# Two weight splits of the second routed expert moved ahead of the slot scatters on GpSimd

## The chip, the cores and the metric

One core of one Trainium2 chip. The metric is device time in microseconds, median of three runs. A profiled execution of the same kernel gives the trace.

## What is computed

Patch embedding, one attention layer and one mixture-of-experts layer over 16 images of 69 tokens (1 class token, 36 patches, 32 text tokens), so T = 1104 tokens of width 256:

```python
h = tok(x)                                   # layernorm, 768 -> 256, layernorm, position table
h = concatenate([h, txt], axis=1)
h = h + attn(layernorm(h))                   # one head, rotary, width 256
n = layernorm(h)
shared = gelu(n @ shared_up) @ shared_down   # 256 -> 1024 -> 256
probs = softmax(n @ router_w)                # 8 experts, top 2
routed = sum over the top 2 of prob * (gelu(n @ up[e]) @ down[e])
out = h + shared + routed + n
```

## The kernel before

The engines run programs of their own and meet at semaphores. Each matrix product in the expert part is done as three products of a high and a low part (split_product, lines 791 to 797), so each weight half of 128x2048 numbers (`w_up` or `w_dn` of one expert) is split on GpSimd once it has landed in `stage`: `hi` is a rounded copy (line 346, tensor_scalar), `lo` the rest (line 347, tensor_tensor). The results go into `ring`, which has RING = 3 places of two halves each. Expert 0 is the shared one, 1 to 8 are routed.

`prepare_half(x, part)` (line 354) splits one half, tells `w_free`, and issues by `load_weights` (line 331) the load of the half that is two further on in the list. At part 1 it also tells `w_ready`, on which TensorE waits before the expert's first product. From x = 3 on it waits first until the place in the ring is free: for x = 3 until the shared expert is done (`ffn_done` of 1), for later ones until the expert three before has had its last tile.

The shared expert is done in 3 groups of 384 tokens by 8 pieces of 128 hidden columns, n = 0 to 23: TensorE makes the up product (shared_up), ScalarE the gelu into `gact` (line 593), VectorE splits it into `hid` (lines 1142 and 1143), TensorE adds the down product (line 844) of three pieces earlier. At the end of each group VectorE adds the result to `base` (line 1151).

Routing is woven into it. VectorE takes the softmax and the two best experts of each token (lines 1210 to 1236; ScalarE does the exp of line 611 in between), TensorE counts tokens before each by 18 small products (line 892), and VectorE makes of them the slot of each token at its expert (lines 1245 to 1260). On its semaphore `r_slots` (line 1260) GpSimd starts 18 scatters (line 477), each of up to 128 token rows from `hx` to `slots` in HBM. SP waits for all of them (line 304) and reads the slots back in tiles of 128 into `xg`.

Then come TILES = 25 routed tiles: TensorE transposes xg and does up, transposes of the hidden tile, and down; ScalarE and VectorE empty PSUM in between (lines 619, 642, 650, 1288, 1311), VectorE scales by the gate into `y_all` (line 1318). GpSimd adds each tile to the output by an accumulating indirect DMA (line 493), in a loop that stands behind all prepare_half calls, and waits between some of them for the earlier ones to have landed.

The order on GpSimd's own queue around the change is written out by hand: split(1, 0), prepare_half(1, 1), the waits for `slots_init` and `r_slots`, the 18 scatters, prepare_half of x = 2 to 8, the additions.

Of the kernel before, what the change touches and what calls it, by code (L numbers as in the profile page):

```python
# [50 lines left out]
NX = NE + 1  # L51
# [8 lines left out]
def fusion_layer(nc, patches, txt, cls_token, cls_pos, ln1_gb, tok_w, tok_bias, ln2_g, ln2_b,  # L60
# [16 lines left out]
    with ctx:  # L77
# [245 lines left out]
        def _(pool):  # L323
# [7 lines left out]
            def load_weights(n):  # L331

                if n < 2 * NX:
                    if n >= 2:
                        pool.wait_ge(w_free, n - 1)
                    pool.dma_start(stage[:, n % 2, :], (w_up, w_dn)[n % 2][n // 2, :, :]).then_inc(w_in[n % 2], 16)

            def tiles_before(x):

                return pool.value_load(tend_int[0:1, x - 1:x], min_val=0, max_val=TILES)  # L340

            def split(x, part, c0, c1):

                pool.wait_ge(w_in[part], 16 * (x + 1))
                hi, lo = (ring[:, x % RING, v, UPW * part + c0:UPW * part + c1] for v in range(2))
                link(nc.gpsimd.tensor_scalar(hi, stage[:, part, c0:c1], 1.0, 0.0, ALU.mult, ALU.add))  # L346
                return nc.gpsimd.tensor_tensor(lo, stage[:, part, c0:c1], hi.bitcast(F32), ALU.subtract)  # L347

            def turn_done(x):

                pool.wait_ge(w_free, 2 * x + 2)
                pool.sem_inc(w_ready, 4)  # L352

            def prepare_half(x, part):

                if x > RING and part == 0:

                    pool.wait_ge(ffn_done, tiles_before(x - RING) + 1)
                    pool.sem_inc(slot_free, 1)
                elif x == RING and part == 0:  # L360

                    pool.wait_ge(ffn_done, 1)
                split(x, part, 0, UPW).then_inc(w_free, 1)
                if part == 1:
                    turn_done(x)
                load_weights(2 * x + part + 2)
# [61 lines left out]
            def flat_bases(g):  # L428
                for i in flat_tiles_after(g):
                    pool.wait_ge(f_normed, i + 1)  # L430
                    r = ROWS[i]
                    nc.gpsimd.tensor_tensor(base[0:r, i, :], h2f[0:r, i % NBUF_FLAT, :], hx[0:r, i, 0:D],
                                            ALU.add).then_inc(f_base, 1)
# [35 lines left out]
            load_weights(4)  # L469
            flat_bases(NG)  # L470
            prepare_half(1, 1)

            pool.wait_ge(slots_init, 32)
            pool.wait_ge(r_slots, 1)
            for i in range(NT):
                for k in range(2):
                    pool.indirect_dma_start(  # L477
                        slots_d, bass.IndirectOffsetOnAxis(ap=slot_i[0:ROWS[i], k, i:i + 1].bitcast(U32), axis=0),
                        hx[0:ROWS[i], i, :], None).then_inc(slots_out, 16)
            for x in range(2, NX):  # L480
                for part in range(2):
                    prepare_half(x, part)

# [892 lines left out]
```

## Time and profile before

| | us |
|---|---|
| median of 3 runs | 402.31 |
| lowest, highest | 398.47, 403.0 |
| profiled execution | 403.5 |
| its span, first to last instruction | 401.5 |

The profiled execution had a mean granted TensorE clock of 0.902 of full speed. In the rows below a line of a timeline has the start in us, the duration in us, engine, line of the program, operation, what is written and read, the count, and in brackets the idle time before it with what ended it.

### The profile page before, as it was taken

Reading aid. Unit: us, or ns where it says so; the run is one execution under the profiler, and the core shown is the slowest. Engines: PE = TensorE matmul, PEld = TensorE weight load, DVE = VectorE, ACT = ScalarE, POOL = GpSimd, SP = SyncE. Lnnn points to the kernel's source line nnn. Section 1 sums busy time; section 2 is a strip of 40 time slices with the busy share of each in tenths; the row PEclk is TensorE's granted clock in tenths of the full one; section 3 lists DMA queues with packets and bytes.
Section 4 is the critical chain, followed back from the end, with each engine's and each line's share of the span. In section 5 each row is a group of like instructions: output and inputs, shape, how many; then the busy total and the mean of one; then the engine's idle time right before and its main releaser. Section 6 shows DMA issues by size and latency. Waiting matters only on the chain.

```text
span 401.5 us, 6810 instructions
## 1 busy us (share of the span) xinstructions
PE 312.3 (78%) x2019; PEld 278.8 (69%) x2020; DVE 229.4 (57%) x494; ACT 118.1 (29%) x239; POOL 239.0 (60%) x164
## 2 busy tenths in 40 slices
PE   0895939865895699808778999989999999999600
PEld 0673837764783499807767898979999999998500
DVE  2588889996779968309696345452475342423200
ACT  1464422511322231100132343424242434343000
POOL 1587548756258804789285058589987755466341
PEclk9999769998697679957898999999999999999965
DMA  8926390411320322225325103335434235344322
GB/s 232 242 54 215 130 288 23 132 49 36 134 89 7 110 93 81 107 84 170 109 73 210 40 15 128 121 120 194 157 118 131 41 43 78 50 52 52 42 26 26
DMA packets 22995, 41.17 MB, mean 103 GB/s; under 512 B 2622, under 2 KB 19456, under 8 KB 20672
## 3 DMA queue, kind: packets, MB, share of 16 engines
q0 software_dynamic: 7056, 24.46, 22.5%
q1 hardware_dynamic: 15264, 15.93, 14.7%
q10 hardware_dynamic: 656, 0.55, 0.4%
q8 instruction: 10, 0.16, 0.2%
q14 instruction: 9, 0.07, 0.1%
HBM read 29.01 MB, written 11.90 MB: 102 GB/s over the span
## 4 chain that ended last, share of the span: by engine, by line
PE 36%; DVE 22%; DMA 20%; issue 8%; POOL 6%; another core or an unknown queue 3%; POOLq 2%; ACT 1%; SPq 0%; DVEq 0%; ACTq 0%
DMA out_tokens<-y_all,dest 10%; PE ps L794 8%; PE ps L795 8%; PE ps L796 8%; DMA h_after_attention<-h 5%; PE ps L660 5%; PE ps L844 5%; DVE hid L1143 4%; DVE hid L1142 2%; POOL ring L347 2%; DMA xp<-in_patches 2%; POOLq L490 2%; DMA h2f<-h_after_attention 2%; DVE qk L1040 1%
## 5 line engine op out<-in xcount | busy, mean ns | idle before, releaser
L347 POOL TENSOR_TENSOR ring<-stage,ring 128x2048 fp32r<-128x2048 f32 (+1 forms) x21 | 84.7, 4032 | 1.8
L493 POOL DMA_INDIRECT out_tokens<-y_all,dest x25 | 39.1, 1565 | 40.5 <-DMA out_tokens<-y_all,dest 33.2
L1311 DVE TENSOR_TENSOR hgT<-ps,hgT 128x512 fp32r<-128x512 f32 x50 | 32.2, 686 | 53.3 <-ACT hgT L650 53.3
L794 PE MATMUL ps<-ring,hgT 128*128 x200 | 58.0, 290 | 2.1 <-DVE y_all L1318 1.5
L346 POOL TENSOR_SCALAR ring<-stage 128x2048 fp32r<-128x2048 f32 (+1 forms) x21 | 36.6, 1742 | 34.5 <-PE ps L796 24.7
L795 PE MATMUL ps<-ring,hgT 128*128 x200 | 56.0, 280 | 0.0
L796 PE MATMUL ps<-ring,hgT 128*128 x200 | 55.9, 280 | 0.0
L844 PE MATMUL ps<-ring,hid 128*128 128x256 f32 x216 | 33.2, 304 | 15.5 <-DVE base L1151 12.1
L642 ACT ACTIVATE hg<-ps 128x512 f32<-128x512 f32 x50 | 29.9, 598 | 51.3 <-PE ps L796 51.3
L794 PE MATMUL ps<-ring,xgT 128*128 x100 | 42.2, 422 | 2.1 <-POOLq L352 1.0
L844 PEld LDWEIGHTS ps<-ring,hid 128*128 128x128 f32 x216 | 31.6, 211 | 16.5 <-issue 12.3
L796 PE MATMUL ps<-ring,xgT 128*128 x100 | 40.2, 402 | 0.0
L795 PE MATMUL ps<-ring,xgT 128*128 x100 | 40.1, 401 | 0.0
L794 PEld LDWEIGHTS ps<-ring,hgT 128*128 128x128 f32 x200 | 37.6, 188 | 2.6 <-issue 2.6
L795 PEld LDWEIGHTS ps<-ring,hgT 128*128 128x128 f32 x200 | 37.6, 188 | 0.0
L796 PEld LDWEIGHTS ps<-ring,hgT 128*128 128x128 f32 x200 | 37.5, 187 | 0.0
L1318 DVE TENSOR_SCALAR y_all<-ps,gate 128x256 f32 (+1 forms) x25 | 12.1, 484 | 39.0 <-PE ps L796 39.0
L593 ACT ACTIVATE gact<-ps 128x384 f32<-128x384 f32 x24 | 11.8, 492 | 65.8 <-DVE hid L1143 25.7
L477 POOL DMA_INDIRECT slots<-hx,slot_i x18 | 17.8, 990 | 21.5 <-DVE tend_int L1260 16.3
L650 ACT ACTIVATE hgT<-ps 128x512 fp32r<-128x512 f32 x50 | 27.1, 598 | 2.6 <-PE ps L660 2.6
L1143 DVE TENSOR_TENSOR hid<-gact,hid 128x384 fp32r<-128x384 f32 x24 | 26.3, 1095 | 0.8
L619 ACT ACTIVATE xgT<-ps 128x256 fp32r<-128x256 f32 x25 | 9.6, 385 | 56.4 <-PE ps L660 56.4
(167 smaller groups left out, 681.0 us busy)
## 6 DMA issues: line engine op xcount, KB each, us to landing
stage<-in_w_up POOLq DMA_DIRECT2D x9, 1024.0 KB, 5.2
stage<-in_w_dn POOLq DMA_DIRECT2D x9, 1024.0 KB, 5.2
slots<-gact SPq DMA_DIRECT2D x1, 3262.5 KB, 14.5
xg<-slots SPq DMA_DIRECT2D x25, 130.5 KB, 2.1
xp<-in_patches SPq DMA_DIRECT2D x6, 288.0 KB, 7.9
h_after_attention<-h SPq DMA_DIRECT2D x4, 276.0 KB
h2f<-h_after_attention SPq DMA_DIRECT2D x8, 128.0 KB, 2.1
ring<-in_tok_w SPq DMA_DIRECT2D x1, 768.0 KB, 6.4
```

The lines of the kernel that those rows point to most:

```text
L346: link(nc.gpsimd.tensor_scalar(hi, stage[:, part, c0:c1], 1.0, 0.0, ALU.mult, ALU.add))
L347: return nc.gpsimd.tensor_tensor(lo, stage[:, part, c0:c1], hi.bitcast(F32), ALU.subtract)
L493: pool.indirect_dma_start(out, bass.IndirectOffsetOnAxis(ap=dest[:, t:t + 1].bitcast(U32), axis=0), y_all[:, t, :], None, compute_op=ALU.a ...
L642: nc.scalar.activation(hg[:, 1 - c, 512 * half:512 * (half + 1)], ps[:, hidden_bank + half, :], ACT.Gelu).then_inc(e_act, 1)
L650: nc.scalar.activation(hgT[:, c, 0, 4 * half:4 * half + 4, :], ps[:, turned_bank + half, :].rearrange("p (k t) -> p k t", k=4), ACT.Copy). ...
L660: return nc.tensor.transpose(o, i, ident[0:n, 0:n])
L794: nc.tensor.matmul(o, a[0], b[0], start=n == 0, stop=False)
L795: nc.tensor.matmul(o, a[0], b[1], start=False, stop=False)
L796: last = nc.tensor.matmul(o, a[1], b[0], start=False, stop=n == len(pairs) - 1)
L844: last = nc.tensor.matmul(ps[:, down_bank[j], 0:D], a[x], b[y], start=f == 0 and m == 0, stop=f == KF - 1 and m == 2)
L1143: v.tensor_tensor(hid[:, 1, f, :], gact[:, n % 2, :], hid[:, 0, f, :].bitcast(F32), ALU.subtract).then_inc(s_lo, 1)
L1311: v.tensor_tensor(hgT[:, c, 1, 4 * half:4 * half + 4, :], ps[:, turned_bank + half, :].rearrange("p (k t) -> p k t", k=4), hgT[:, c, 0, 4 ...
```

## The change

Both halves of expert 2 are split directly behind those of expert 1, ahead of the waits for `slots_init` and `r_slots` and ahead of the scatters. The loop behind the scatters begins at expert 3. With each half the issue of a load moves too: that of `w_up[3]` and of `w_dn[3]`. No wait and no operation is added or dropped.

```diff
             flat_bases(NG)
             prepare_half(1, 1)
+            prepare_half(2, 0)
+            prepare_half(2, 1)
 
             pool.wait_ge(slots_init, 32)
             pool.wait_ge(r_slots, 1)
@@
-            for x in range(2, NX):
+            for x in range(3, NX):
                 for part in range(2):
                     prepare_half(x, part)
```

## Rows read from the trace of the kernel before

**Rows 1.** Timeline of GpSimd, the last expert's splits, the first and last addition
```profile
303.43 1.90 POOL L346 TENSOR_SCALAR ring<-stage 128x2048 fp32r<-128x2048 f32 x1 [2.05 <-PE ps L796]
...
311.99 4.61 POOL L347 TENSOR_TENSOR ring<-stage,ring 128x2048 fp32r<-128x2048 f32 x1
317.56 1.68 POOL L493 DMA_INDIRECT out_tokens<-y_all,dest  x1 [0.96 <-DVE y_all L1318]
...
394.64 1.56 POOL L493 DMA_INDIRECT out_tokens<-y_all,dest  x1 [2.86 <-DMA out_tokens<-y_all,dest]
```

**Rows 2.** Timeline of VectorE, the last tile of y
```profile
379.46 0.48 DVE L1318 TENSOR_SCALAR y_all<-ps,gate 128x256 f32<-128x256 f32 x1 [4.15 <-PE ps L796]
```

**Rows 3.** Timeline of TensorE, its one wait for weights in the routed tiles
```profile
269.58 0.49 PE L794 MATMUL ps<-ring,xgT 128*128 x1 [1.02 <-POOLq L352]
```

**Rows 4.** Timeline of GpSimd, 133 to 209 us: splits, load, scatters
```profile
133.50 4.53 POOL L347 TENSOR_TENSOR ring<-stage,ring 128x2048 fp32r<-128x2048 f32 x1
138.62 0.60 POOL L336 DMA_DIRECT2D stage<-in_w_dn  x1 [0.59 <-POOL ring L347]
155.53 1.17 POOL L477 DMA_INDIRECT slots<-hx,slot_i  x1 [16.31 <-DVE tend_int L1260]
...
177.62 0.90 POOL L477 DMA_INDIRECT slots<-hx,slot_i  x1 [0.30 <-issue]
...
188.06 4.56 POOL L347 TENSOR_TENSOR ring<-stage,ring 128x2048 fp32r<-128x2048 f32 x1
...
203.92 4.63 POOL L347 TENSOR_TENSOR ring<-stage,ring 128x2048 fp32r<-128x2048 f32 x1
```

**Rows 5.** The page, DMA issues: count, size, median from issue to landing
```profile
stage<-in_w_dn POOLq DMA_DIRECT2D x9, 1024.0 KB, 5.2
```

**Rows 6.** Timeline of VectorE beside GpSimd's splits, and once without
```profile
133.66 4.78 DVE L1143 TENSOR_TENSOR hid<-gact,hid 128x384 fp32r<-128x384 f32 x1
...
139.61 0.56 DVE L1143 TENSOR_TENSOR hid<-gact,hid 128x384 fp32r<-128x384 f32 x1
...
188.23 4.80 DVE L1143 TENSOR_TENSOR hid<-gact,hid 128x384 fp32r<-128x384 f32 x1
...
204.08 0.35 DVE L1299 TENSOR_REDUCE ytab<-ecmp 1x25 f32<-1x200 f32 x1
204.47 4.13 DVE L1300 SCALAR_TENSOR_TENSOR ytab<-small,rtab 1x25 f32<-1x25 f32 x1
```

**Rows 7.** Timeline of VectorE, the routing chain up to the slot numbers
```profile
142.48 0.23 DVE L1220 TENSOR_TENSOR rout<-rout,rsm 128x72 f32<-128x72 f32 x1
...
145.90 0.17 DVE L1236 TENSOR_SCALAR hx<-rsm 128x9 f32<-128x9 f32 x1
...
151.35 0.17 DVE L1245 COPY rtab<-ps 128x8 f32<-128x8 f32 x1 [0.18 <-PE ps L892]
...
154.45 0.16 DVE L1260 CAST tend_int<-rtab 1x8 int32<-1x8 f32 x1
```

**Rows 8.** Timeline of TensorE: the counting products, two restarts after idle time, the last shared products
```profile
149.20 2.11 PE L892 MATMUL ps<-rsel,mats 128*128 128x72 f32 x18
...
182.44 2.26 PE L844 MATMUL ps<-ring,hid 128*128 128x256 f32 x9 [12.05 <-DVE base L1151]
...
193.08 2.29 PE L844 MATMUL ps<-ring,hid 128*128 128x256 f32 x9 [2.40 <-DVE hid L1143]
...
200.45 1.30 PE L844 MATMUL ps<-ring,hid 128*128 128x256 f32 x9
```

**Rows 9.** Windows of TensorE: length, busy (instructions), granted clock, DMA share, GB/s
```profile
182.40:186.00 3.60, 3.56 (x14) 0.50 0.59 184
...
193.00:196.50 3.50, 3.42 (x14) 0.52 0.54 169
```

**Rows 10.** Timelines of ScalarE and of VectorE, the stall inside the scatters
```profile
179.74 0.49 ACT L593 ACTIVATE gact<-ps 128x384 f32<-128x384 f32 x1 [10.77 <-remote]
...
181.21 1.08 DVE L1151 TENSOR_TENSOR base<-base,ps 128x256 f32<-128x256 f32 x3 [11.26 <-remote]
```

## The prediction

> **What bounds the kernel now.** I read the page first, then the timelines of GpSimd, VectorE, TensorE and ScalarE between 120 and 215 us, then the tail, because the page shows no engine full over the whole span and the reader has to find, stretch by stretch, which one the others wait for.
>
> The tail belongs to GpSimd. It issues the 25 accumulating DMAs of line 493 only when all weight splits are done: the last split starts at 311.99 us and takes 4.61, the first addition starts at 317.56 and the last at 394.64 [rows 1]. VectorE had the last tile of y ready at 379.46 + 0.48 us [rows 2], 15 us before its addition, and the same holds for every addition before it, so the additions are a fixed string of 77 us hung on the end of the splits. The splits of the eighth routed expert start at 303.43 us, after 2.05 us of idling for TensorE [rows 1]: they wait for the last tile of the fifth. TensorE runs tile behind tile up to there, with one wait worth a name, 1.02 us at 269.58 [rows 3]. So what moves the start of the routed phase moves the end one to one. That start is the end of the shared expert (201.75 us: 200.45 + 1.30, the last products of line 844 [rows 8]), followed by a stretch in which VectorE is held up behind the split of expert 3, which is itself released by the end of the shared expert. Everything hangs on when TensorE finishes the shared expert.
>
> Before that lies the routing: VectorE's chain of small operations to the slot numbers (line 1260 at 154.45), 18 scatters on GpSimd from 155.53 to 178.52, one each 1.27 us [rows 4], and then x = 2's two splits, which this change moves.
>
> **What is removed, added, moved.** Nothing is removed. Two halves of work move to the front of the wait for the slot numbers. Each is a tensor_scalar of 1.90 us [rows 1] and a tensor_tensor of 4.5 us [rows 4], with the load of the half after the next (0.60 us of issue [rows 4]). Their data are there: the first half was requested before the splits of expert 1 ended, the second at 138.62 [rows 4], and such a load lands 5.2 us after its issue [rows 5]. From 139.26 I get: first tensor_scalar to 141.2, tensor_tensor 141.25 to 145.8, 0.3 gap, issue to 146.7, second pair 146.75 to 148.66 and 148.75 to 153.3, wait and issue to 154.5. That is 15.2 us in an idle gap of 16.31 us [rows 4]. On GpSimd alone the edit costs nothing, since the slot numbers come 154.6 us; with that cover gone it would cost up to 15.2 us. The two extra loads (7 and 6 of the list) move ahead of the scatters with it; they use the queue while nothing else does, and their 5.2 us are over before the first scatter. SP's queue is passed by nothing; what waits on it for the scatters are the reads of xg.
>
> **The cost: VectorE while GpSimd splits.** Three operations show it. VectorE's line 1143 (two inputs from SBUF) takes 0.56 us alone, 4.78 us at 133.66 beside GpSimd's tensor_tensor of 133.50, and 4.80 at 188.23 beside that of 188.06; it ends 0.4 us after GpSimd's [rows 4, 6]. Small size does not save it: the 1x25 operation of line 1300 takes 4.13 us at 204.47 and ends with the split of 203.92 (4.63 us). The tensor_reduce of line 1299 at 204.08, inside that same split, takes 0.35 and is not held [rows 4, 6]. The Trainium skill (SBUF — State Buffer, Who interferes with whom) says the same of two-input operations and of reduces; it adds that who issues first keeps the port and the other waits, which is a rival below.
>
> So I walk VectorE's chain through the four new GpSimd operations, letting one held operation in at each boundary. Line 1142 of n = 7 (139.22 before) ends at 141.4. Its line 1143 waits for 145.8 and ends at 146.2. The maximum and the subtraction (lines 1210, 1211; input from PSUM) run, ScalarE's exp answers, lines 1213 and 1214 run; line 1215 has two SBUF inputs and waits for 148.66; line 1219 is a reduce; line 1220 waits for the last split and ends at 153.5. Before, it ended at 142.71 [rows 7]. From there nothing holds the chain: +10.8 us. The mask (end of line 1236, 146.07 before [rows 7]) is at 156.9.
>
> TensorE's 18 small products of line 892 took 2.11 us at full clock from 149.20 [rows 8]. They now start at 157.0, after TensorE has idled some 5 us: its shared steps run out of finished pieces at about 151.4, as n = 8 of ScalarE also waits behind the late exp. After idle times of 12 and 2.4 us the granted clock was 0.50 and 0.52 (1.2 GHz) for the next 3.5 us [rows 8, 9]; at that clock the products take 4.4 us and end at 161.4. The other end, full clock, gives 159.3. I take the slow one. VectorE's line 1245 moves from 151.35 to 161.6: **+10.2 us** (other end 8.3), and so do the slot numbers (154.61 to 164.8) and the scatters: 165.7 to 188.7.
>
> **The stall inside the scatters.** Between about 170 and 180 us ScalarE, VectorE and TensorE all stand still. ScalarE idles 10.77 us until 179.74, VectorE 11.26 us until 181.21, both on an unnamed releaser, though the products they need ended at 167.2 and 168.3 by the trace [rows 10]; TensorE waits 12.05 us for VectorE [rows 8]. It ends about 1.2 us after GpSimd's last scatter (177.62 + 0.90). No row names the cause. I take it to belong to the scatters, since it begins well inside them and ends with them: the change then shifts it whole, to 190-191. TensorE's distance from its line 892 to the first scatter stays 4.3 us, so it gets as far before the stall as now.
>
> **The gain.** After the stall TensorE needs 182.44 to 201.75 = 19.3 us. In it lie 2.40 us of waiting for line 1143, held by the second half's split, and then 3.5 us at clock 0.52 [rows 8, 9], which loses half of them, 1.7. With the splits gone from there both vanish: **-4.1 us**, leaving 15.2. The other holds of VectorE in this stretch lie under TensorE's slow-clock work and pay nothing. TensorE ends the shared expert at 192.6 + 15.2 = 207.8 instead of 201.75. Tiles 0 and 1 of xg are there by then: read from about 191.4 on, and even at the 5.2 us of the larger weight load [rows 5] landed by 197. Expert 2's weights are ready at 154 instead of 194, but TensorE asks for them only after the tiles of expert 1, and it has no wait there now: no gain. GpSimd waits for TensorE at the split of expert 3 before and after, so the earlier end of the splits is idle time there.
>
> **Sum:** +10.2 - 4.1 = +6.1 us on the span of 401.5, so 407.6; the profiled execution was 403.5 and the median of three is 402.31, which makes 408.4 by the latter. About 1% (4 us) is what a measurement of this kernel can tell.
>
> **Rivals.**
> A, the forecast, 0.56: 408.4. With full clock at line 892: +8.3 - 4.1 = +4.2, 406.5. If TensorE is one shared step (2.1 us) less far when the stall begins: 410.5. Own range 405.5 to 411.
> B, the stall does not come back, 0.13: TensorE goes on from 161.4 with 13 steps of 2.1 us (line 844's nine products take 2.26 at half clock [rows 8], so 1.1 at full, the up products as long) and three lone down products, 3.4 us: 192.4. It must also have xg: scatters end 188.7, and a larger load lands in 5.2 [rows 5], so at most 193.9, then two down products, 196. I take 194.5, between these, against 201.75. -7.2 us, 395.1. For it: the stall has no named releaser; against it: the same scatters run beside the same work. It decides the sign as soon as more than 6 of the 12 us are gone.
> C, VectorE is first at the port and keeps the chain moving, 0.12: the chain's operations take 0.23 us, and if each is let in ahead of GpSimd, the slot numbers come as now, and only the -4.1 remains: 398.2. For it: VectorE's operations are many and short; against it: in every case in rows 4 and 6 the VectorE operation waited for the whole of GpSimd's. The page of the skill named above supports either, by order of issue, and gives no price here.
> D, between, 0.19: the holds cost half (some small operations slip in, or line 1220 falls into the gap of 0.9 us between the halves), or part of the stall is absorbed: +5 - 4.1 or +10.2 - 10: about 0 to +3.5, 402 to 406.
>
> **Numbers.** The likeliest is 408.4. Above 411.5 I leave 0.07, below 397.5 0.10 (most of B): range 397.5 to 411.5. Slower by over 1%: nearly all of A and some of D, 0.55. Within 1%: most of D, the mild edge of A and of C, 0.22. Faster: B, most of C, 0.23.
>
> **What would show it.** In the changed profile: four GpSimd splits between 139 and 154; line 1143 of n = 7 near 4.9 us and line 1220 near 4.7; line 1245 near 161.6; TensorE's line 892 at about twice 2.1 us; first scatter near 165.7; a stall of about 10 us on ScalarE ending near 190; no wait of TensorE for line 1143 after it; first split of expert 3 near 208; first addition near 323.6. Wrong if line 1260 stays under 158 (C), or if ScalarE has no unnamed wait over 5 us (B).

## The result

The changed kernel takes 407.36 us (median of 4, 405.68 to 409.7), the kernel before 401.34 (median of 4, 398.47 to 403.0): ratio 1.0138, 95% interval 1.0084 to 1.0192, so about 6 us slower. In a later pair of the same two programs it was 405.2 against 400.31, ratio 1.0145 (1.0063 to 1.0227). All medians here take every execution, while the ratios leave out those over 1.5% above the fastest of their kernel, so a ratio can differ a little from the quotient of the medians beside it.

The profiled execution of the changed kernel is its fastest one, 405.68, with a span of 403.7 us, against 401.5 before: 2.2 us in the two traces for 6 us in the medians. That gap needs an explanation of its own, below.

The lines that were added move the ones below: what was line 1142 is 1144 here, 1143 is 1145, 1220 is 1222, 844 is 846, 890 is 892, 892 is 894, 1283 is 1285. First GpSimd's timeline, to be read beside [rows 4]: start, duration, operation, and idle time before it.

```profile
139.25 1.91 POOL L346 TENSOR_SCALAR ring<-stage 128x2048 fp32r<-128x2048 f32 x1
141.25 4.76 POOL L347 TENSOR_TENSOR ring<-stage,ring 128x2048 fp32r<-128x2048 f32 x1
146.31 0.58 POOL L336 DMA_DIRECT2D stage<-in_w_up  x1 [0.30 <-POOL ring L347]
146.92 1.91 POOL L346 TENSOR_SCALAR ring<-stage 128x2048 fp32r<-128x2048 f32 x1
148.92 4.55 POOL L347 TENSOR_TENSOR ring<-stage,ring 128x2048 fp32r<-128x2048 f32 x1
...
165.61 1.17 POOL L479 DMA_INDIRECT slots<-hx,slot_i  x1 [10.97 <-DVE tend_int L1262]
...
187.44 0.90 POOL L479 DMA_INDIRECT slots<-hx,slot_i  x1 [0.30 <-issue]
207.72 1.90 POOL L346 TENSOR_SCALAR ring<-stage 128x2048 fp32r<-128x2048 f32 x1 [19.38 <-PEq L908]
```

The splits fit into the former gap, but GpSimd still idles 10.97 us for the slot numbers, and the first scatter is 10.1 us later. The time saved on GpSimd behind the scatters appears as 19.38 us of waiting for the shared expert. VectorE's timeline shows what made the slot numbers late (beside [rows 6, 7]):

```profile
138.77 2.81 DVE L1145 TENSOR_TENSOR hid<-gact,hid 128x384 fp32r<-128x384 f32 x1
141.50 4.73 DVE L1144 CAST hid<-gact 128x384 fp32r<-128x384 f32 x1
...
148.08 0.84 DVE L1217 TENSOR_TENSOR rout<-rout,rsm 128x72 f32<-128x72 f32 x1
148.96 0.23 DVE L1221 TENSOR_REDUCE rsm<-rout 128x9 f32<-128x72 f32 x1
149.22 4.33 DVE L1222 TENSOR_TENSOR rout<-rout,rsm 128x72 f32<-128x72 f32 x1
...
161.44 0.17 DVE L1247 COPY rtab<-ps 128x8 f32<-128x8 f32 x1 [1.82 <-PE ps L894]
```

Each held operation ends 0.1 to 0.4 us after the GpSimd operation beside it (141.58, 146.23, 148.92 and 153.55 against 141.16, 146.01, 148.83 and 153.47); a product of 72 numbers per partition takes 4.33 us instead of 0.23, and the reduce between two held ones takes its 0.23. The longest hold, 4.73 us, is of a cast, which has only one SBUF input. TensorE, beside [rows 8]; the line ACT is ScalarE's gelu of n = 16, with the stall in front of it:

```profile
156.97 0.71 PE L892 MATMUL ps<-rsel,mats 128*128 128x80 f32 x2 [5.13 <-DVE hx L1238]
157.47 3.93 PE L894 MATMUL ps<-rsel,mats 128*128 128x72 f32 x18
...
185.69 0.49 ACT L595 ACTIVATE gact<-ps 128x384 f32<-128x384 f32 x1 [9.46 <-remote]
186.33 0.66 PE L796 MATMUL ps<-hT_n,ring 128*128 128x384 f32 x1 [6.66 <-issue]
...
194.06 1.26 PE L846 MATMUL ps<-ring,hid 128*128 128x256 f32 x9 [0.70 <-DVE base L1153]
...
206.23 1.30 PE L846 MATMUL ps<-ring,hid 128*128 128x256 f32 x9
```

The counting products take 3.93 us, not 2.11, at a granted clock of 0.50 (157 to 161.5 us) behind an idle time of 5.13. The shared expert is done at 207.53, 5.8 us later than before (201.75). From 194.06 on no wait for line 1145 is left.

### The profile page after: what moved, and what is told of

It reads as the page before. It is cut to its first block, busy times and chain, and to the rows that moved or that the text cites. A ratio compares the mean times of both kernels' runs of the same rounds, so it can differ in the third digit from the quotient of the medians.

```text
span 403.7 us, 6810 instructions
## 1 busy us (share of the span) xinstructions
PE 314.8 (78%) x2019; PEld 280.5 (69%) x2020; DVE 227.2 (56%) x494; ACT 117.9 (29%) x239; POOL 238.9 (59%) x164
## 4 chain that ended last, share of the span: by engine, by line
PE 35%; DVE 24%; DMA 19%; issue 7%; POOL 6%; another core or an unknown queue 4%; POOLq 2%; ACT 1%; SPq 0%; DVEq 0%; ACTq 0%
DMA out_tokens<-y_all,dest 10%; PE ps L796 8%; PE ps L798 8%; PE ps L797 8%; DMA h_after_attention<-h 5%; PE ps L662 5%; PE ps L846 4%; DVE hid L1145 4%; POOL ring L347 2%; DVE hid L1144 2%; POOLq L492 2%; DMA xp<-in_patches 2%; DMA h2f<-h_after_attention 2%; DVE qk L1042 1%
## 5 line engine op out<-in xcount | busy, mean ns | idle before, releaser
L796 PE MATMUL ps<-ring,xgT 128*128 x100 | 41.6, 416 | 2.2 <-POOLq L352 1.0
L797 PE MATMUL ps<-ring,xgT 128*128 x100 | 39.5, 395 | 0.0
L798 PE MATMUL ps<-ring,xgT 128*128 x100 | 39.5, 395 | 0.0
L1144 DVE CAST hid<-gact 128x384 fp32r<-128x384 f32 x24 | 15.6, 651 | 25.7 <-issue 13.1
L796 PE MATMUL ps<-hT_n,ring 128*128 128x384 f32 x48 | 20.0, 416 | 9.3 <-issue 6.9
```

The source lines that it names most:

```text
L796: nc.tensor.matmul(o, a[0], b[0], start=n == 0, stop=False)
L797: nc.tensor.matmul(o, a[0], b[1], start=False, stop=False)
L798: last = nc.tensor.matmul(o, a[1], b[0], start=False, stop=n == len(pairs) - 1)
L1144: link(v.tensor_copy(hid[:, 0, f, :], gact[:, n % 2, :]))
```

## Why the traces differ by 2 us and the medians by 6

I looked at what lies between the end of the shared expert and the first y (line 1318): 19.6 us in the trace before (201.75 to 221.34), 15.75 in the changed one (207.53 to 223.28). Both hold the same operations. The first two lines are VectorE's and TensorE's of the kernel before:

```profile
208.93 2.47 DVE L1283 SCALAR_TENSOR_TENSOR junk<-xg,etab 128x2 f32<-128x2 f32 x1
...
211.95 0.41 PE L660 MATMUL ps<-mats,xg 128*128 128x128 f32 x2 [2.77 <-DVE xgT L1288]
```

and these the changed kernel's:

```profile
214.68 0.21 DVE L1285 SCALAR_TENSOR_TENSOR junk<-xg,etab 128x2 f32<-128x2 f32 x1
...
215.44 0.41 PE L662 MATMUL ps<-mats,xg 128*128 128x128 f32 x2 [0.43 <-DVE xgT L1290]
```

A tiny operation of VectorE meets the gap between two GpSimd operations of expert 3's split. In the one trace it was held for 2.47 us; TensorE then idled 2.77 us, and from 212.90 to 216.60 its granted clock was 0.57. In the other it took 0.21 us. The two traces hardly differ in their times there: the operation starts 0.08 us after GpSimd's load issue in both, and GpSimd's next operation 0.54 us after it in the one and 0.59 in the other. So I call it a race, but what decides it is not seen. It hid 3.8 of the 5.8 us. A second trace of the kernel before, taken beside a second one of the changed kernel, won the race too, so the same program can lose it or win it:

```profile
199.78 1.31 PE L844 MATMUL ps<-ring,hid 128*128 128x256 f32 x9
...
208.23 0.21 DVE L1283 SCALAR_TENSOR_TENSOR junk<-xg,etab 128x2 f32<-128x2 f32 x1
...
216.87 0.48 DVE L1318 TENSOR_SCALAR y_all<-ps,gate 128x256 f32<-128x256 f32 x1 [1.29 <-PE ps L796]
```

Its partner has the shared expert done at 206.66 and the first y at 222.44: +5.57 us at both places, spans 402.7 and 398.8. Of the 5.57, 1.7 are lost again in the string of additions, which took 78.8 us from first to last in the one and 77.2 in the other (77.1 and 77.3 in the first two traces, 79.1 in half_moved below). This spread of 2 us, in a string that waits for its DMAs to land, is why a single span can't be trusted.

## The experiments

The experiments ran on three chips, and these are not alike: the kernel before took 402.78 and 400.31 us in two groups of runs on the first, 392.54 on the second, 402.06 on the third. The second and the third chip were used in one group of runs each, so what is said of a chip below could also belong to that group. Each kernel is compared with the kernel before on its own chip.

**Half of the move.** Only prepare_half(2, 0) goes ahead of the waits.

```diff
             prepare_half(1, 1)
+            prepare_half(2, 0)
...
-            for x in range(2, NX):
+            prepare_half(2, 1)
+            for x in range(3, NX):
```

> Only the first half of expert 2 is split ahead of the waits; the second half stays behind the scatters. Theory (each held operation of VectorE's routing chain costs what its GpSimd neighbour lasts, and TensorE's clock falls only if it idles some us): line 1220 is no longer held, so the mask comes near 152.2 instead of 156.9, TensorE idles under 1 us before the counting products and does them at full clock, the first scatter is near 159.2 (165.6 with both halves, 155.5 with none). The split behind the scatters still holds VectorE, but only under TensorE's slow restart. Shared expert done near 201.3, time about 401, within 1% of before. Rival (the cost is proportional to the work moved): half of +6, 404.3.

Measured: 400.5 us against 402.78, ratio 0.997 (0.992 to 1.0019). VectorE and TensorE of this kernel:

```profile
147.53 0.23 DVE L1217 TENSOR_TENSOR rout<-rout,rsm 128x72 f32<-128x72 f32 x1
...
148.06 0.23 DVE L1222 TENSOR_TENSOR rout<-rout,rsm 128x72 f32<-128x72 f32 x1
...
151.99 2.11 PE L894 MATMUL ps<-rsel,mats 128*128 128x72 f32 x18
```

The first scatter is at 158.44, some 3.7 us later than in the second trace of the kernel before on this chip (154.78), where both halves cost 10, and the shared expert is done at 200.54 against 201.09. TensorE restarts behind the stall at 185.35, 3.6 us later than there (181.73), and then needs 15.2 us instead of 19.4: the gain of 4.1 is whole, and it pays for the 3.6. The cost is not in proportion to the work moved: the second half holds line 1222 and thereby also puts TensorE to half clock. Half the move costs nothing measurable; both halves cost 6 us. The rival's 404.3 falls.

**GpSimd busy, but not reading.** The moved operations are replaced by memsets of the same ring halves, so expert 2's weights are zero and its share of the output is left out.

```diff
             def split(x, part, c0, c1):
...
+                if x == 2:
+                    link(nc.gpsimd.memset(hi.bitcast(F32), 0.0))
+                    for _ in range(2):
+                        link(nc.gpsimd.memset(lo.bitcast(F32), 0.0))
+                    return nc.gpsimd.memset(lo.bitcast(F32), 0.0)
```

> The changed kernel, but for expert 2 the four moved GpSimd operations are replaced by memsets of the same ring halves (one for the high, three for the low part of each half): GpSimd is busy at the same place and writes as much or more, but reads nothing from SBUF. Expert 2's weights are so all zero and its share of the output is left out. Theory (VectorE's two-input operations wait for a GpSimd operation that reads SBUF, and for nothing else of it): lines 1217 and 1222 take 0.23 us each, the copy of line 1144 may still be held once or twice; the first scatter is at 157 to 159, not at 165.6. Rival (any busy GpSimd, or the loads it issues, delays the chain): the first scatter is near 165.

Measured: GpSimd was busy with memsets of 1.8 to 2.0 us each from 138.08 to 154.05, and VectorE went on beside them. The lines of VectorE are the cast of n = 7, what was line 1220, and an operation of 9 numbers and the next cast; the last line is GpSimd's.

```profile
138.09 2.03 DVE L1149 CAST hid<-gact 128x384 fp32r<-128x384 f32 x1
...
142.50 0.23 DVE L1227 TENSOR_TENSOR rout<-rout,rsm 128x72 f32<-128x72 f32 x1
...
145.95 2.33 DVE L1243 TENSOR_SCALAR hx<-rsm 128x9 f32<-128x9 f32 x1
146.02 2.45 DVE L1149 CAST hid<-gact 128x384 fp32r<-128x384 f32 x1
...
155.91 1.21 POOL L484 DMA_INDIRECT slots<-hx,slot_i  x1 [0.75 <-issue]
```

What is held here has one SBUF input: two casts, the operation of 9 numbers (0.17 us in [rows 7]) and, later, the cast of a slot number for 0.99 us. No operation with two SBUF inputs is held by a memset. The first scatter is at 155.91; on the same chip the three kernels with nothing moved ahead of the scatters have it at 153.57, 154.33 and 154.87. So 1 to 2.3 us are left of the 10, and the loads, which are issued here as well, are cleared: it is GpSimd's reading of SBUF that holds VectorE's operations with two SBUF inputs. The Trainium skill (SBUF — State Buffer, Who interferes with whom) states this rule, that two SBUF inputs contend only with a GpSimd operation that reads SBUF; these rows bear it out, with 0.23 us beside a memset for 4.33 beside a split. The whole kernel took 385.77 us, a single execution.

**The race taken out, before and after.** prepare_half(3, 0) waits for line 1303 as well, in both kernels.

```diff
                     pool.wait_ge(ffn_done, 1)
+                    pool.wait_ge(r_additions, 1)
```

> The kernel before, and the split of expert 3 waits besides for the last small operation of VectorE's table for the additions (line 1303). In the profile of before, a small operation of line 1283 was held by that split from 208.93 to 211.40, TensorE waited 2.77 us and then ran at half clock to 216.6; in the profile of the changed kernel the same operation took 0.21 us and TensorE waited 0.43. Theory (a race of tenths of a us between the two, lost in some executions and won in others, hides part of the change in the one profile): without it the first y is ready about 13.5 to 14.5 us after the end of the shared expert in place of 19.6, and the median falls by 3 to 5 us, to about 397. Rival (the hold is under other work): no change.

Measured: 398.25 us against 402.78, ratio 0.9918 (0.9869 to 0.9967). The first y comes 14.2 us behind the end of the shared expert (200.68 to 214.86), as expected, against 15.8 where the race is won and 19.6 where it is lost. So the added wait is worth 1.6 us in the one case and 5.4 in the other, and the median fell by 4.5, more than where the race is won: the kernel before seems to lose the race in most of its executions, which is an inference from medians, not seen in traces.

> The changed kernel with the same added wait ahead of the split of expert 3. Theory: the cost of the change is all spent before the end of the shared expert, so this stands 6 us above late3_before, about 403, and its profile shows the whole 6. Rival (the 2.2 us between the two profiles' spans are what the change costs): 2 us above late3_before.

Measured: 405.38 us, 7.1 above late3_before; shared expert done at 207.23 against 200.68 (+6.55), first y at 221.41 against 214.86 (+6.55). With the race out, trace and medians agree: the change costs 6 to 7 us, nearly all of it before the end of the shared expert. The changed kernel hardly gains by the added wait (405.38 against 407.36 and 405.2), and both of its own traces have the race won.

**Nothing of expert 2 before the shared expert is done.**

```diff
+            pool.wait_ge(r_additions, 1)
             for x in range(2, NX):
```

> The kernel before, with the splits of expert 2 and all later ones behind a wait for line 1303, so that neither VectorE's routing chain nor its shared pieces nor the table for the additions are held by a split. GpSimd idles from 178.5 to about 204 and does experts 2 and 3 in one go until about 235, when expert 1's place comes free. Theory: TensorE's 2.40 us wait and the second half-clock stretch vanish (-4.1) and so does the race (-3 to -5): about 393.5. Rival (expert 2 comes too late for its first tile, or expert 4 is delayed by a busy GpSimd): a wait of TensorE for w_ready and a time near or above 398.

Measured: 397.36 us against 402.78, ratio 0.986 (0.9701 to 1.0019), near the rival's 398, and the rival's wait for weights came. TensorE restarts at 183.54 and is done with the shared expert at 198.92: 15.4 us for the 19.3 of before, so the -4.1 of the forecast is 3.9. But TensorE then stood for expert 2's weights, 2.5 us by its products (2.8 by the weight loads ahead of them), and y of tile 1 came 9.52 us after tile 0 instead of 6.72. I had put the first use of expert 2's weights at the end of expert 1's tiles; TensorE asks for them one to two tiles earlier, since it makes the up product two tiles ahead of the down product. In the forecast nothing hung on it.

**One half early, one late.** The first half of expert 2 stays behind the scatters; the second half and expert 3 go behind the wait.

```diff
+            prepare_half(2, 0)
+            pool.wait_ge(r_additions, 1)
+            prepare_half(2, 1)
-            for x in range(2, NX):
+            for x in range(3, NX):
```

> The kernel before, with the first half of expert 2 split behind the scatters as before, and the second half and expert 3 behind the wait for line 1303. In late2, TensorE stood 2.8 us for expert 2's weights (y of tile 1 came 9.52 us after tile 0, not 6.72). Theory: here the weights are ready near 209, before TensorE asks for them, the hold of TensorE (2.40 us and the half clock behind it) is gone as in late2: near 394.5. Rival (what late2 gained came from elsewhere): near late3_before, 398.

Measured: 386.18 us against 392.54 on the same chip, ratio 0.983 (0.9814 to 0.9847), 6.4 us less, between the 8 of the theory and the 4.5 of the rival (late3_before). The absolute figure is of another chip than late2's; the ratios, 0.983 and 0.986, can't be told apart by late2's interval. No product waits for weights. And ScalarE shows no stall inside the scatters at all:

```profile
168.74 0.49 ACT L596 ACTIVATE gact<-ps 128x384 f32<-128x384 f32 x1 [1.63 <-PE ps L799]
171.25 0.49 ACT L596 ACTIVATE gact<-ps 128x384 f32<-128x384 f32 x1 [2.02 <-PE ps L799]
173.37 0.49 ACT L596 ACTIVATE gact<-ps 128x384 f32<-128x384 f32 x1 [1.63 <-PE ps L799]
...
182.49 0.69 PE L663 MATMUL ps<-mats,xg 128*128 128x128 f32 x2 [2.83 <-DMA xg<-slots]
```

The gelus follow every 2.1 to 2.5 us through the time in which [rows 10] has 10.77 us of nothing. TensorE waits here for xg, 2.83 us (last line). The other three kernels run on this chip show none either, write_only and paced with all 18 scatters and half_scatters with 9. So the stall does not belong to the program alone, and that may be most of the 10 us between the kernel before on this chip and on the others.

**Half the scatters.** Only k = 0, and additions strictly in turn so that they stay ordered; the second choice's share of the output is left out. SP waits for 9 scatters instead of 18.

```diff
-                for k in range(2):
+                for k in range(1):
...
-                    pool.wait_ge(y_out, pool.value_load(additions[0:1, t:t + 1], ...))
+                    pool.wait_ge(y_out, 16 * t)
```

> The kernel before with only the 9 scatters of each token's first choice (the second expert's share of the output is left out), and with the additions at the end strictly one behind the other, so its total time says nothing; read it between 155 and 205 us. Theory (the stall of ScalarE, VectorE and TensorE belongs to the later half of 18 back-to-back scatters and ends with them): the scatters end near 167, no unnamed wait over 3 us stands on ScalarE, TensorE comes to its first down product of the third group near 171 to 173 in place of 182.44, and the shared expert is done near 190. Rival (the stall belongs to a place in the engines' instruction streams): a wait near 10 us at the same gelu (the nineteenth) remains, shared expert done near 200.

It ran on the chip without the stall: no unnamed wait, first down product of the third group at 167.63. That decides nothing. So again:

> half_scatters once more (only the 9 scatters of the first choice, additions strictly one behind the other, so the total says nothing), since the first time it ran on a chip where the kernels with all 18 scatters do not show the stall either. On the chip with the stall, ScalarE's unnamed wait began 13 us after the first scatter and ended about 1 us after the last. Theory (the stall belongs to the later part of a long row of scatters): with 9 of them, over after 12 us, ScalarE shows no unnamed wait over 3 us, the first down product of the third group starts near 170 in place of 181.7. Rival (it belongs to a place in the instruction streams): a wait near 10 us at the nineteenth gelu.

Measured, on a third chip where the kernel before took 402.06: no unnamed wait on ScalarE. TensorE's group starts at 174.49 where 170 was expected, because VectorE was held by expert 2's split, which now comes as early as 166:

```profile
173.44 0.49 ACT L593 ACTIVATE gact<-ps 128x384 f32<-128x384 f32 x1 [4.90 <-DVE hid L1143]
...
174.49 2.26 PE L844 MATMUL ps<-ring,hid 128*128 128x256 f32 x9 [4.89 <-DVE base L1151]
```

With half the scatters the stall is not there; no trace of the unchanged kernel from this chip exists, so that it would be there with all 18 rests on its time, and on the next run, which has a short one on this chip. Its scatters are also over at 166.3, before the stall of the other traces begins.

**A pause in the row.** As one_early_one_late, but the first half is split between the 8th and the 9th scatter.

```diff
             for i in range(NT):
+                if i == 4:
+                    prepare_half(2, 0)
                 for k in range(2):
```

> As one_early_one_late, but the first half of expert 2 is split between the 8th and the 9th scatter, which puts about 7 us without scatters into their row and ends them near 185.5 in place of 178.5. Theory (the stall comes of many scatters close behind each other): it becomes shorter than 10 us or splits, and the shared expert is done earlier than in one_early_one_late, near 192 to 196: about 390. Rival (it ends with the last scatter, whatever is between): ScalarE stands until about 187, TensorE's restart is 7 us later: about 401.

On the chip without the stall: 388.79 us against 392.54, ratio 0.991 (0.9884 to 0.9937), 2.6 us slower than one_early_one_late, as the scatters and with them xg come later. Once more on the third chip:

> paced once more for the same reason (first half of expert 2 split between the 8th and the 9th scatter, second half and expert 3 behind the wait for line 1303). Theory (it takes a long unbroken row of scatters): on the chip with the stall, ScalarE's unnamed wait is under 5 us in sum, the shared expert is done near 193, and the time is 392 to 394 against 401 for the kernel before. Rival (it ends with the last scatter, whatever is between): ScalarE stands until about 186, the shared expert is done near 202, the time is 398 to 400.

Measured: 389.32 us against 402.06, ratio 0.9759 (0.9662 to 0.9856). ScalarE's timeline:

```profile
179.55 0.49 ACT L597 ACTIVATE gact<-ps 128x384 f32<-128x384 f32 x1 [1.63 <-issue]
185.92 0.49 ACT L597 ACTIVATE gact<-ps 128x384 f32<-128x384 f32 x1 [5.87 <-remote]
187.47 0.49 ACT L597 ACTIVATE gact<-ps 128x384 f32<-128x384 f32 x1 [1.06 <-remote]
```

The stall is 5.87 us long (6.9 with the 1.06 behind it, over the 5 that I gave it, and over half of the first chip's 10.8 and 1.1). On the second chip the same program has none. It begins 7 us after the first scatter of the second row of ten (173.08) and ends 0.2 us after the last scatter (184.82 + 0.90); the shared expert is done at 193.44, as the theory had it, while the stall still ends with the last scatter, as the rival had it. The pause was not tried by itself on a chip with the stall, since one_early_one_late did not run there: how much of the gain is the pause's, and how much the late second half's, is open. This version beats the kernel before with the stall and without it; the changed kernel did not run on these two chips.

**The same pair once more, with a trace of each.**

> The changed kernel as it is, beside the kernel before on a chip of its own. On one chip the kernel before took 402.8 us and every kernel on it showed the stall of ScalarE, VectorE and TensorE inside the scatters; on another it took 392.5 and none of the kernels with 18 scatters showed a wait of ScalarE over 5 us on an unnamed releaser. Theory: with the stall (a kernel before near 402) the change costs 6 us as forecast. Without it (near 392) the shared expert goes on during the scatters, and xg, which comes about 4 us after the last scatter, is what TensorE waits for: the scatters are 10.2 us late either way, so the change costs more than with the stall, 6 to 9 us, since the wait for VectorE that it removes lies before that wait for xg. Rival: without the stall it costs nothing or gains.

> The kernel before once more, for a trace of it from the same chip. Theory: if its time is near 392, no unnamed wait over 5 us on ScalarE between 155 and 182, the first down product of the third group near 169 to 171 in place of 182.44, and TensorE held later by VectorE's line 1143 beside the splits of expert 2. If it is near 402, the rows are those of the first trace. Rival (the chips differ elsewhere): a time near 392 with the stall in it.

Measured: 405.2 against 400.31 us, and the pair of traces told above. It was the first chip again, with the stall: ScalarE waits 10.78 us on an unnamed releaser until 179.03 in the kernel before (last scatter to 177.79), and 9.36 until 186.20 in the changed one (last scatter to 187.86), followed by 3.84 us until 190.53 for an up product. What the change costs on a chip without the stall was not tried.

## Why the prediction was right, point by point

- The holds. Forecast: line 1143 of n = 7 to 146.2, line 1220 to 153.5, mask at 156.9. Measured: 146.27 + 0.56, 149.22 + 4.33 = 153.55, mask at 156.75 + 0.17. I had put the hold of n = 7 on its line 1143; it was one operation earlier, line 1143 of n = 6 for 2.81 us (which I had left free) and the cast of n = 7 for 4.73, while line 1143 of n = 7 took its 0.56 in the gap. So my sign "line 1143 of n = 7 near 4.9 us" did not come. The end is the same, since each ends with its GpSimd neighbour.
- The clock at line 892. Forecast 4.4 us at half clock, 161.4; measured 0.71 and 3.93, end 161.40. The full-clock end, 159.3, falls. First scatter forecast 165.7, measured 165.61.
- The stall. It went along with the scatters, as in A: ScalarE waits 9.46 us until 185.69 and 5.26 more until 191.45, where it was 10.77 and 1.06 before. TensorE's 6.66 us until 186.33 look like a stall of its own, as the trace names no releaser, but the program has a wait there: the up product of n = 18 waits for the gelu of n = 16, which ends at 185.69 + 0.49 = 186.18. What TensorE shows of its own are gaps of 0.2 to 1.0 us inside groups of nine products without any wait between them (0.78 at 179.27 here, 1.01 in late3_after). I had forecast equal progress ahead of the stall; TensorE was one down group and two up products less far (the 2.1 us that I had as the edge of A), because half clock lasted beyond the counting products (0.50 from 161.4 to 165.3). These were done by fits from 186.3 on. The restart with down products of group 3 is at 194.06, not 192.6.
- The gain. Forecast 15.2 us from the restart, measured 13.5 (194.06 to 207.53). The work left is the same at both restarts, but TensorE had run by fits from 186.3 on and was at full clock (1.00 from 193 to 208) when this one came; my 15.2 still had the 3.6 us at clock 0.50 of [rows 9] in it. The two misses, +1.5 and -1.7, cancel, and that the sum is so close is luck to that extent. The term -4.1 for the hold behind the scatters was 3.9 in late2 and 4.1 in half_moved.
- Sum. Forecast +6.1; measured at the end of the shared expert +5.8, +5.57 and +6.55 in three pairs, medians +6.0, +4.9 and +7.1 (the third pair is the one with the added wait).
- What I did not see: that the trace before had lost a race worth 3.8 us. I had taken its 19.6 us between shared expert and first y for fixed. It did not hurt, since the forecast goes by the difference and the medians mix both outcomes, but my "first addition near 323.6" came out 319.50. A fit of trace to trace would have read 2 us.
- Rivals. C (VectorE first at the port) has nothing for it: both two-input operations of the chain that met a split waited for its end. D (half the holds) did not come: the slot numbers are 10.1 us later. B (no stall) did not happen in the measured trace, but on another chip the stall is absent, in every kernel that left a trace there; so it was a rival of the chip rather than of the change, and the kernel before is itself faster there (392.54), which my sum for B left out. Its sum of 192.4 should read 192.1 (161.4 + 27.3 + 3.4); nothing hangs on it.

## What to carry over

An idle gap on GpSimd is not free when VectorE has a chain of small dependent operations in it: here each one with two SBUF inputs that met a split operation waited for its end, and so did a cast, so that 13 us of splits cost 10 us of chain. Put such splits where VectorE reduces, has an input in PSUM or waits (line 1213 of the changed kernel, with one input in PSUM, took its 0.23 us at 147.01 beside a split), or move just as much as ends before the chain begins: half of this move cost nothing. And compare more than one trace of each kernel before a difference of 1% is explained: one tiny operation, held in one execution and let through in another, was worth 3.8 us here.

## What was not expected of the hardware

During a long row of scatters from GpSimd, ScalarE stands still without a named releaser: its longest such wait is 8.0 to 10.8 us in the first measurement and on the first chip. In the kernel before VectorE does so too, for 11.26, and TensorE waits for it. On another chip this does not happen at all (392.54 us against 400 to 403 for the same program). In the nine traces that have it, ScalarE's last wait of this kind ends between 1.7 us before and 3.1 us after the end of the last scatter, and moves with the row (from 180.1 to 191.5 us). It is missing with 9 scatters, and is 5.87 us when 7 us of other work stand in the row (these two on the third chip). What it is made of stays open: no releaser is named, and no trace of DMA or engine shows what the engines wait for. TensorE's gaps of up to 1.0 us between products without waits could come from the supply of instructions, which is argued, not shown: in the trace of the kernel before, the fetches of instructions that it has lie between 158 and 160 us and between 196 and 198, none in the stall.
